# A one-core graph network layer: relation-weight bases combined eight per tile pair, and the second copy of the adjacency matrix added to each slab in SBUF

## What is computed

```python
w = jnp.einsum('rb,bio->rio', att, basis)        # 2 relations, 30 bases of 512x512
x_j = x[col]
for r in range(NUM_RELATIONS):
    gate = jax.nn.sigmoid(x_j @ gate_w[r, :, 0])
    msgs.append(gate[:, None] * x_j @ w[r])
msg = jnp.where((edge_type == 0)[:, None], msgs[0], msgs[1])
agg = jax.ops.segment_sum(msg, row, num_segments=x.shape[0])
return agg + x @ root + bias
```

## Time and profile before

| what | us |
|---|---|
| median of 3 runs | 2761.16 |
| lowest and highest run | 2752.94 and 2769.96 |
| span of the profiled execution | 2754.8 |
| TensorE busy | 2409.9 (87%) |
| VectorE busy | 1468.9 (53%) |
| GpSimd busy | 1036.3 (38%) |
| chain that ended last | TensorE 67%, VectorE 13%, DMA 8% |

### The profile page before, as it was taken

How to read it: one execution, slowest core, us unless ns; L and a number is a source line. 1 busy time by engine, 2 the same in 40 slices (tenths; PEclk the granted TensorE clock), 3 DMA queues, 4 the chain that set the end, 5 groups by cost and what they waited for, 6 DMA issues and landing times.

```text
span 2754.8 us, 27581 instructions
## 1 busy us (share of the span) xinstructions
PE 2409.9 (87%) x9500; PEld 1234.4 (45%) x9500; DVE 1468.9 (53%) x3793; ACT 681.1 (25%) x1687; POOL 1036.3 (38%) x885
## 2 busy tenths in 40 slices
PE   3999989997999999999999987889879879875665
PEld 2656656665444444445656654433333333331210
DVE  3765675455666300002345614477677677677664
ACT  1346231211110011002364211223322332321222
POOL 0066877760111000000000000566666656666665
PEclk9999999998999999999999998999999999987856
DMA  9934145478466601440005000799999989989998
GB/s 304 297 64 127 2 109 117 98 157 223 160 181 196 154 1 52 108 112 19 1 1 172 1 8 8 267 327 342 337 327 342 335 316 348 333 317 340 341 358 313
DMA packets 235969, 524.42 MB, mean 190 GB/s; under 512 B 99362, under 2 KB 99737, under 8 KB 231675
## 3 DMA queue, kind: packets, MB, share of 16 engines
q0 software_dynamic: 170032, 379.99, 42.2%
q1 hardware_dynamic: 57477, 137.07, 16.2%
q10 hardware_dynamic: 8330, 5.71, 0.7%
HBM read 489.51 MB, written 45.34 MB: 194 GB/s over the span
## 4 chain that ended last, share of the span: by engine, by line
PE 67%; DVE 13%; DMA 8%; issue 5%; POOL 3%; another core or an unknown queue 2%; ACT 1%; SPq 0%; DVEq 0%; POOLq 0%; ACTq 0%
PE bank L1070 12%; PE bank L1325 6%; PE bank L1047 5%; PE bank L905 4%; PE bank L916 4%; PE bank L1305 4%; PE bank L1315 3%; PE bank L1259 3%; PE bank L678 3%; PE bank L792 3%; PE bank L570 3%; PE bank L584 2%; PE bank L1057 2%; PE bank L577 2%; DMA qv<-in_L_ffn_rows,qv 2%
## 5 line engine op out<-in xcount | busy, mean ns | idle before, releaser
L1228 POOL DMA_INDIRECT qv<-in_L_ffn_rows,qv x356 | 360.1, 1012 | 1009.4 <-issue 909.0
L1448 ACT ACTIVATE stage<-stage,qv 128x32 f32<-128x32 f32 x640 | 200.3, 321 | 576.8 <-issue 199.0
L1325 PE MATMUL bank<-qv,stage 128*32 128x512 f32 x712 | 257.6, 699 | 91.6 <-ACT stage L1448 48.4
L1612 DVE SCALAR_TENSOR_TENSOR qv<-qv,wreg 128x512 f32<-128x512 f32 x356 | 262.8, 746 | 118.2 <-DMA qv<-in_L_ffn_rows,qv 98.0
L284 POOL DMA_INDIRECT adj<-e_cnt,e_idx x80 | 163.7, 2046 | 193.7 <-issue 176.4
L284 POOL DMA_INDIRECT adj_b<-e_cnt,e_idx x80 | 167.3, 2091 | 62.5 <-issue 35.3
L1305 PE MATMUL bank<-stage,big 128*128 128x250 f32 x640 | 174.2, 399 | 7.5 <-ACT stage L1407 7.5
L1228 POOL DMA_INDIRECT big<-in_L_ffn_rows,qv x142 | 145.8, 1027 | 88.1 <-PE bank L1325 40.5
L1315 PE MATMUL bank<-big 128*125 128x512 f32 x320 | 173.0, 633 | 2.1 <-issue 2.1
L1070 PE MATMUL bank<-big,wreg 125*125 125x512 f32 x400 | 172.0, 592 | 0.0
L1070 PE MATMUL bank<-big,qv 125*125 125x512 f32 x400 | 171.8, 592 | 0.0
(11 more groups left out here) (227 smaller groups left out, 3984.8 us busy)
## 6 DMA issues: line engine op xcount, KB each, us to landing
wreg<-in_L_gnn_basis SPq DMA_DIRECT2D x30, 1024.0 KB
stage<-in_L_gnn_basis POOLq DMA_DIRECT2D x45, 512.0 KB, 4.5
big<-in_L_mix_W SPq DMA_DIRECT2D x4, 4096.0 KB
adj<-adj_b POOLq DMA_DIRECT2D x9, 1328.1 KB, 37.5
adj<-wreg SPq DMA_DIRECT2D x5, 2187.5 KB
adj_b<-wreg SPq DMA_DIRECT2D x5, 2187.5 KB
wreg<-adj SPq DMA_DIRECT2D x10, 1093.8 KB
qv<-adj SPq DMA_DIRECT2D x10, 1093.8 KB
```

The costliest lines, as they stand in the source:

```text
L1228: nc.gpsimd.indirect_dma_start(out=ring[place(t, s)], out_offset=None, in_=a["L0_ffn_rows"], in_offset=bass.IndirectOffsetOnAxis(ap=slots_ ...
L1325: nc.tensor.matmul(psum[7][WIDE * g:WIDE * g + WIDE, :], wsel[:, s % DRING, :], ring[place(t, s)][:, DIM:ROW], start=(s < 4), stop=(s >= S ...
L1448: nc.scalar.activation(wsel[:, s % DRING, :], mask, ACT.Relu, scale=inner[:, s:s + 1]).then_inc(p_diag, 1)
L1612: nc.vector.scalar_tensor_tensor(ring[place(t, s)][:, 0:DIM], ring[place(t, s)][:, 0:DIM], probs_of[t % 2][:, s:s + 1], xrep[:, s % 4, :], ...
```

## The change

Three things. (1) `combine` takes 8, 8, 8, 6 and 0 bases in the five pairs, four of them ahead of the next pair's `norm2`; the loops are written out. (2) The ten sums in device memory are gone. Each slab is loaded from `adj` into SBUF, and then GpSimd adds the same rows of `adj_b` to it there by an accumulating DMA; TensorE waits for that one. This is done for each of the 10 slabs in both layers. (3) The half bases are loaded by SyncE, in its program order between the loads of `gx` and of the slabs, and are spread as 4 per tile in the z stage and then 3, 2, 3, 2, 3, 2, 3, 2. The first two slabs of layer 1 are loaded at tile 7 of the z stage.

```diff
-            for n in range(2):
-                pool.wait_ge(s_adj[n], GROUPS // 2 * 16)
-            for n in range(SUMS):
-                rows = slice(272 * n, min(272 * n + 272, CELLS // 1250))
-                nc.gpsimd.dma_start(adj_rows[rows, :], adj_b_rows[rows, :], accum_op=ALU.add, max_dma_last_dim=5000).then_inc(s_sum, 16)
...
+        BASES_AT = ((0, 4, 8), (8, 12, 16), (16, 20, 24), (24, 28, 30), (30, 30, 30))
...
+            for i in range(PAIRS):
+                b0, b1, b2 = BASES_AT[i]
+                combine(b0, b1 - b0)
+                if i < PAIRS - 1:
+                    norm2(dve, 0, i + 1)
+                combine(b1, b2 - b1)
                 ffn_take(dve, 0, i)
...
             sp.dma_start(b_g, a[f"L0_gnn_bias{gl + 1}"].partition_broadcast(P)).then_inc(g["b"], 16)
-            if gl == 0:
-                for t in range(2, TILES):
-                    sp.wait_ge(g["xT_pe"], t - 1)
-                    sp.dma_start(gx[:, t % 2, :], tok(xn_d)[:, t, :]).then_inc(s_gx[t % 2], 16)
...
             if gl == 0:
-                sp.wait_ge(s_sum, 16 * SUMS)
-            load_slab(0)
-            load_slab(1)
-            if gl == 1:
+                half_bases_sp(sp, 0, HRING)
+                for t in range(TILES):
+                    half_bases_sp(sp, HALVES_AT[t] + HRING, HALVES_AT[t + 1] + HRING)
+                    if t + 2 < TILES:
+                        sp.wait_ge(g["xT_pe"], t + 1)
+                        sp.dma_start(gx[:, t % 2, :], tok(xn_d)[:, t + 2, :]).then_inc(s_gx[t % 2], 16)
+                    if t == SLABS_AT:
+                        for n in range(2):
+                            sp.wait_ge(s_adj[n], GROUPS // 2 * 16)
+                        load_slab(0)
+                        load_slab(1)
+                for t in range(TILES):
+                    half_bases_sp(sp, HALVES_AT[TILES + t] + HRING, HALVES_AT[TILES + t + 1] + HRING)
+                    if t + 2 < TILES:
+                        sp.wait_ge(g["agg"], t + 1)
+                        load_slab(t + 2)
...
-                pe.wait_ge(s_slab[gl][j], 32 * (t // 2) + 32)
+                pe.wait_ge(s_slabsum[gl][j], 32 * (t // 2) + 32)
...
+        def half_bases_sp(sp, first, until):
+            for n in range(first, min(until, 2 * BASES)):
                 if n >= HRING:
-                    pool.wait_ge(s_half, 2 * (n - HRING) + 2)
+                    sp.wait_ge(s_half, 2 * (n - HRING) + 2)
...
+        def slab_sums_pool(pool, gl):
+            for t in range(TILES):
+                flat = slabs[gl][:, t % 2, :, :].rearrange("p c r -> p (c r)")
+                pool.wait_ge(s_slab[gl][t % 2], 32 * (t // 2) + 32)
+                for rows in ROWS:
+                    nc.gpsimd.dma_start(flat[rows, :], adj_b_t[t, rows, :], accum_op=ALU.add, max_dma_last_dim=5000).then_inc(s_slabsum[gl][t % 2], 16)
...
-        HALVES_AT = [3 * t for t in range(TILES)] + [3 * TILES + 4 * t for t in range(8)] + [2 * BASES] * 3
+        HALVES_AT = [4 * t for t in range(TILES)] + [4 * TILES + (5 * t + 1) // 2 for t in range(8)] + [2 * BASES] * 3
```

More of the change, by code:

```diff
@@ L69, in build @@
         adj_t = adj[0:CELLS, :].rearrange("(t p n) o -> t p (n o)", p=P, n=COLT * P)
-        adj_rows, adj_b_rows = (x[0:CELLS, :].rearrange("(a n) o -> a (n o)", n=1250) for x in (adj, adj_b))
-        SUMS = -(-CELLS // (1250 * 272))
+        adj_b_t = adj_b[0:CELLS, :].rearrange("(t p n) o -> t p (n o)", p=P, n=COLT * P)
         def tok(ap):
@@ L435, in bases_sp @@
             sp.sem_inc(s_comb, 2 * BRING)
[L436 to L441, removed]
+            for b in range(BASES):
+                sp.wait_ge(s_comb, 2 * b + 2)
+                sp.dma_start(wreg[:, b % BRING, :].rearrange("p (k n) -> p k n", k=KC),
+                             a["L0_gnn_basis1"][b].rearrange("(k p) n -> p k n", p=128)).then_inc(s_basis[b % BRING], 16)
         KD_BANKS = (4, 5, 6, 7)
@@ L871, in mlp_dve, with combine @@
             dve.wait_ge(s_comb0, 2)
[L873 to L876, removed]
+            def combine(first, count):
+                for b in range(first, first + count):
+                    dve.wait_ge(s_basis[b % BRING], 16 * (b // BRING) + 16)
+                    dve.wait_ge(s_comb, 2 * b + 2 * BRING)
                     for r in range(RELS):
-                        nc.vector.scalar_tensor_tensor(wrel[:, 0, r, :], wreg[:, n % BRING, :], att_b[:, 0, ds(i * BLOCKS + (r * BASES + n), 1)],
+                        nc.vector.scalar_tensor_tensor(wrel[:, 0, r, :], wreg[:, b % BRING, :], att_b[:, 0, r * BASES + b:r * BASES + b + 1],
                                                        wrel[:, 0, r, :], ALU.mult, ALU.add).then_inc(s_comb, 1)
[L881 to L884, removed]
+            for i in range(PAIRS):
[4 more added lines that the diff above has]
+                combine(b1, b2 - b1)
                 ffn_take(dve, 0, i)
-            combine(PAIRS - 1, range(BLOCKS))
-            ffn_take(dve, 0, PAIRS - 1)
             dve.wait_ge(m["hf"], 2 + 2 * TILES)
@@ L956, in build @@
         s_slab = [[sem(f"gcn{gl}_slab_{j}") for j in range(2)] for gl in range(2)]
+        s_slabsum = [[sem(f"gcn{gl}_slab_summed_{j}") for j in range(2)] for gl in range(2)]
+        SLABS_AT = 7
         COMB_DONE = 2 * BRING + 2 * BASES
@@ L989, in gcn_sp @@
             if gl == 0:
-                sp.wait_ge(s_sum, 16 * SUMS)
-            load_slab(0)
-            load_slab(1)
-            if gl == 1:
+                half_bases_sp(sp, 0, HRING)
[14 more added lines that the diff above has]
+                        load_slab(t + 2)
+            else:
+                load_slab(0)
+                load_slab(1)
                 sp.wait_ge(g["r"], TILES)
@@ L997, in gcn_sp @@
                 attn_vectors(sp, 1)
-            for t in range(2, TILES):
-                sp.wait_ge(g["agg"], t - 1)
-                load_slab(t)
+                for t in range(2, TILES):
+                    sp.wait_ge(g["agg"], t - 1)
+                    load_slab(t)
         def gcn_x_act(act, gl):
@@ L1091, in gcn_act @@
                         turned(t + 1)
-        def half_bases_pool(pool):
-            pool.wait_ge(m["hat"], 2 + 2 * TILES)
-            for n in range(2 * BASES):
+        def half_bases_sp(sp, first, until):
+            for n in range(first, min(until, 2 * BASES)):
                 if n >= HRING:
-                    pool.wait_ge(s_half, 2 * (n - HRING) + 2)
+                    sp.wait_ge(s_half, 2 * (n - HRING) + 2)
                 k0 = 2 * (n % 2)
-                nc.gpsimd.dma_start(half_ring[n % HRING].rearrange("p (k n) -> p k n", k=2),
-                                    a["L0_gnn_basis2"][n // 2].rearrange("(k p) n -> p k n", p=128)[:, k0:k0 + 2, :]).then_inc(s_hload[n % HRING], 16)
+                sp.dma_start(half_ring[n % HRING].rearrange("p (k n) -> p k n", k=2),
+                             a["L0_gnn_basis2"][n // 2].rearrange("(k p) n -> p k n", p=128)[:, k0:k0 + 2, :]).then_inc(s_hload[n % HRING], 16)
+        def slab_sums_pool(pool, gl):
[4 more added lines that the diff above has]
+                    nc.gpsimd.dma_start(flat[rows, :], adj_b_t[t, rows, :], accum_op=ALU.add, max_dma_last_dim=5000).then_inc(s_slabsum[gl][t % 2], 16)
         def half_bases_dve(dve, first, count):
@@ L1673, in _ @@
             adjacency_pool(pool)
-            half_bases_pool(pool)
+            slab_sums_pool(pool, 0)
+            slab_sums_pool(pool, 1)
             mem_pool(pool)
```

2 lines of the change are left out of this document (removed).

## The result

| | before | after |
|---|---|---|
| median, us | 2761.32 (2752.94 to 2769.96) | 2814.03 (2812.65 to 2820.0) |
| span of the profiled execution, us | 2754.8 | 2812.9 |
| end of the MLP to first transpose, layer 1 | 13.32 idle | none |
| z stage of layer 1, start to first aggregation | 681.7 to 802.9 | 667.0 to 803.2 |
| aggregation of layer 1, without the 11.6 behind it | 172.3 | 205.8 |

The ratio is 1.019 [1.017, 1.022]: slower by 53 us, outside the range forecast. All of it arises before the end of graph layer 2, +60.8 by the two traces; the rest took 1492.4 us before and 1489.7 after.

A forecast was written before the change was run, and what follows sets the result against it. TensorE was taken as the bound, so only a hole of 17.3 us could be won; -17.3 + 9.7 + 4 + 2 + 2 + 3 = +3.4, added to the median: 2765 us, forecast 2756 to 2771, range 2746 to 2800.

The forecast's parts named there:

- part 3: Both aggregations: load then sum of each slab, chain 16.2 us against 17.17; +2 for layer 1, +3 for layer 2.
- 17.17: Aggregations: us per tile, the deadline for everything put between the end of tile t and the start of tile t+2.
- company: Traffic beside the slab sums: chain 17.4 in layer 1 with half loads, 17.6 in layer 2 with ACT's store and load.
- Slabs 0 and 1: Layer 1: loaded at tile 7, some 23 us before need; 6.3 + 9.8 plus two half loads' overlap fits.
- the price of a miss: Aggregations: chain over the deadline costs 0.2 to 0.7 per pair of tiles; +2 layer 1, +3 layer 2 (0 to 11 each).
- Rival (a): Aggregations: slower addition into SBUF, slab ring off its beat; chain 20.5 gives +38, 2803 (2780 to 2815); chance 0.24.
- The hole of 17.3 us: MLP's end to layer 1's first transpose: 13.3 idle plus 4 of half clock, all that can be won; -17.3.
- The `xn` load of tile 2: Layer 1's z stage: `gx` 2 stands behind half loads on SyncE; TensorE waits +9.7, with +4 of half clock after.
- later tiles: Layer 1's z stage: `gx` loads land 0.3 us late in each of seven tiles, +2 (0 to 9).
- Part 1: MLP: eight bases per pair, all in at about 590, so TensorE goes on at 668.4 without the hole; -17.3.
- the odd slabs: Layer 2's aggregation, a sign: groups released by the sum DMA at odd slabs rather than even ones.
- A chain's excess: Aggregations: with two buffers, a chain C over the deadline costs C - 17.17 per pair of tiles, not per tile.

The follow-up runs named there:

- a ring of four: Changed kernel with four slab buffers, `xn` loads ahead of half loads, and layer 1's slabs 0 to 3 loaded early; ratio 0.994 to before.
- Parts 1 and 2 together: Changed kernel with the slab sums undone: ten sums in device memory again, eight bases per pair and SyncE half loads kept; ratio 1.001 to before.
- The third experiment: Changed kernel with six bases per pair instead of eight, slab sums and SyncE half loads kept; ratio 1.019 to before.
- part 1 without part 3: Kernel before with only the bases combined 8, 8, 8, 6, 0, sums still in device memory and half bases on GpSimd; ratio 0.996 to before.

## Why the prediction was wrong

**The step that failed** is part 3's "Sum 6.3 + 0.1 + 9.8 = 16.2 us against 17.17: it fits with 1 us to spare". With company it was to be 17.4 to 17.6; the chains measured are 17.9 without company and 20.4 in the mean. Three things were in it, each too small.

First the chain by itself. I took the load's end 1 us behind the end of its traffic in the earlier trace rows. Slab 8 of the change is a load with nothing beside it: asked for at 937.27, traffic until 943, and GpSimd's wait ends at 944.97.

```profile
942.00:943.00 1.00, 1.00 (x4) 0.45 (x3) 1.00 (x2) 0.00 (x0) 0.00 (x0) 1.00 0.99 220
943.00:944.00 1.00, 1.00 (x3) 0.38 (x2) 0.21 (x1) 0.00 (x0) 0.00 (x0) 1.00 0.02 0
944.00:945.00 1.00, 1.00 (x4) 0.48 (x3) 0.00 (x0) 0.00 (x0) 0.03 (x1) 1.00 0.00 0
```

```profile
944.97 2.01 POOL L1112 DMA_DIRECT2D wreg<-adj_b  x2 [14.60 <-DMA wreg<-adj]
```

That is 7.7 us, of which two pass between the last byte and GpSimd's going on. The Trainium skill, "DMA: Bandwidth & Descriptors", section "Anatomy of one DMA — SWDGE (gpsimd) path", has it that the receipt of the last byte makes up most of the fixed 2 us; it says so of GpSimd's DMAs, and these rows show the same on SyncE's. The sum of this slab had nothing beside it either. The view of the DMA queues, 945 to 955 us, has its second transfer, which GpSimd issued 0.7 us after it went on:

```profile
wreg<-adj_b POOLq DMA_DIRECT2D x1, 127.0 KB, 9.5
```

So the sum took 10.2 where I had 9.8: the neighbour in device memory was a good price, and what I had left out is that a slab's sum is issued as two transfers, one after the other. Alone, 7.7 + 10.2 = 17.9 us is over 17.17 already. The estimate of 4.9 us for the whole slab, worked out in the prediction from the fit of the same section of the Trainium skill, is not borne out.

Second the company. I had 1.2 us of it in layer 1 and 1.4 in layer 2, from "the accumulating one got 82%". Sums beside half loads took up to 12.0, those beside ACT's transfers 12.5 to 13.2, the one beside layer 2's first loads 23.7. The 82% of the earlier trace rows was a ratio between queues of 5000-byte and 2 KB pieces; the slab loads have rows of 10000 bytes, and beside such pieces the share was 42% to 61%, with the packets one for one in both. The rule of the Trainium skill, "DMA: Bandwidth & Descriptors", section "Queues, rings and completion order", that an engine alternates between its queues packet by packet, agrees with both; I had used the result of one case where the rule called for the piece size of the other. It does not explain the 7 us in which the sum asked for at 964.3 moved nothing. And the load of layer 2's root and slabs at the very slab that is last in layer 1 was in the code and not in my sum: 15.8 of the 24.9 us, and 18.4 of the aggregation with its clock. Slabs 0 and 1 were under-priced too: loaded "some 23 us before need", they were said to fit, but load and sum of slab 0 took from 774.97 to 803.12, 28.2 us, and TensorE waited 3.69.

Third the price of a miss. Above the deadline I put 5 us in all, at full clock. The nine regular gaps (all but that of 15.8) are 27.6 us together, and the clock cost the two aggregations 17. A chain of 17.9 alone would be 0.7 over for each of eight pairs, an estimated 6 us, so most of the 27.6 is company. Rival (a) had the slab ring falling off its beat, the point of 17.2 from which it decides, a chain of 20.5 (20.4 measured) and 27 us of gaps with 16 of clock: 2803 against 2814.03; what it lacks is about the gap of 15.8. Its reason was another, though, an addition that is slower in SBUF than in device memory. That was not so, and that its 20.5 is met is luck. It deserved more than 0.24: the margin of 1 us stood on two rows from other transfers, either of which could be off by more than that.

**What held.** The hole of 17.3 us closed, and a ring of four won it in full. The `xn` load of tile 2 came late by 10.28 where 9.7 was predicted, from SyncE's order of waits; later tiles lost 0.24 + 1.16 = 1.4 for 2; the z stage was 14.7 us earlier at its start and 0.3 later at its end. Parts 1 and 2 together were forecast at -17.3 + 15.7 = -1.6 and measured +1 [-5, +8]; that they agree is in part luck, since the turn of tile 2 waited 18.04 us there and not 9.7. In layer 2 the odd slabs were those that waited from slab 5 on; slab 4 waited 0.44, and slab 2 5.54, its load taking 11.42 us behind the next attention's weights. A chain's excess was paid once for a pair of tiles, as predicted: the gaps of over 1 us stand two or more tiles apart in all but one place (slabs 4 and 5 of layer 1).

**What was right for another reason.** Part 1 was credited with the hole. The third experiment shows that part 3 closes it without part 1; and part 1 without part 3 leaves 8.74 us of it to `xn`. The prediction's own sentence, "The waits were the sums' doing", was the better guide than the list of what is late.

**Open:** how much of layer 1's regular gaps, 9.1 us, the half loads beside the chain cost. They stood beside single loads and sums that took longer (9.12 and 12.0 against 7.7 and 9.5), but no run took them away with the sums kept.

## What to carry to other kernels

A step put between "buffer free" and "next use" has a deadline of (buffers - 1) times the work on one buffer; add what passes between the last byte and the next engine's going on (2 us behind a load here) and the issue of each transfer, and look for what else moves in that time. A margin of 6%, as here, was none: there was a gap for most pairs of tiles, and mostly half clock behind it. With two more buffers, loads asked for early and `xn` ahead of the half loads, the same 20 sums went from +53 us to -17, though in the median they took longer. Before crediting an edit with a closed hole, ask who opened it: two edits that close one hole add up to one, and one that only moves the culprit's traffic moves the hole. And look at what the next stage asks for at the moment when the last buffer of this one is being filled.

## What the runs showed of the hardware

- A slab's sum into SBUF, 1.25 MB by two accumulating DMAs (112 and 13 rows of 10000 bytes in pieces of 5000), took 10.2 us alone from GpSimd's going on, 9.5 from the issue of the second, against 10.3 for 1.36 MB into device memory.
- From the end of a slab load's traffic to the going on of the engine that waited for it 2 us passed.
- Two queues with work moved one packet each in turn: 362 to 364 packets and 82% to 22% of the engines at 5000 bytes against 2 KB, 98 to 103 packets and 42% to 61% at 5000 against mostly 10000-byte rows. Ahead of that, the accumulating queue moved nothing for some 7 us while SyncE's held all engines.
- In the aggregations of all the profiles, gaps of 1.91 to 3.42 us were followed sometimes by 1.2 GHz and sometimes by 2.4; behind every gap of 3.45 us and more it fell, and behind none of 1.89 and less. In the change 43.4 us of gaps within the aggregations went with 17 us more in clock.
- Splitting ACT's 125-row transfers in 112 and 13 rows gave the aggregation beside them 13.6 us back.
